# Reordered work around the half rounds of an RWKV-6 attention and expert kernel, and a fourth of the layer norm on another engine

## The reference, cut to what matters

```python
xn = layernorm(x)                            # x: 4 x 1024 x 256, float32
out = x + attention(xn) + experts(xn)

# attention, RWKV-6: 4 heads of 64
x_last = xn shifted by one token
h = tanh((xn + (x_last - xn) * miu_x) @ A)   # the codes, 5 x 32
x5 = xn + (x_last - xn) * (h @ Bp + lam)     # five mixtures: w, k, v, r, g
w = td_miu + tanh(x5[0] @ tdA) @ tdB
k = x5[1] @ Wk.T * exp(min(w, 0));  v = x5[2] @ Wv.T;  r = x5[3] @ Wr.T
g = tanh(x5[4] @ Wg1) @ Wg2
y_t[i] = sum_j r_t[j] * (S[i,j] + u[j] * k_t[j] * v_t[i])
S[i,j] = S[i,j] * exp(w_t[j]) + k_t[j] * v_t[i]
attention = (groupnorm(y) * gamma + beta) * g @ Wo.T

# experts: 8, each token goes to one
e = argmax(softmax(xn @ Wr + br))
experts = (relu(xn @ W1[e] + b1[e]) @ W2[e] + b2[e]) * max_prob
```

## Time and profile before

| | before |
|---|---|
| median of 3 runs | 611.93 us (611.58 to 612.84) |
| the profiled execution: its time, its span | 612.62 us, 611.3 us |
| PE busy | 545.2 us, 89% of the span |
| PE's weight loads busy | 483.0 us, 79% |
| DVE busy | 449.7 us, 74% |
| ACT busy | 339.4 us, 56% |
| POOL busy | 187.7 us, 31% |
| PE in the chain that ended last | 61% of the span |

### The profile page before, as it was taken

One profiled execution on the slowest core, in us unless ns is written; L12 is line 12 of the kernel. 1 busy time (PEld: TensorE's weight loads), 2 busy tenths in 40 slices (PEclk: granted clock), 3 DMA queues, 4 the chain that ended last, 5 costly groups with the idle time before them and its releaser, 6 DMA issues.

```text
span 611.3 us, 18795 instructions
## 1 busy us (share of the span) xinstructions
PE 545.2 (89%) x7278; PEld 483.0 (79%) x7278; DVE 449.7 (74%) x1124; ACT 339.4 (56%) x753; POOL 187.7 (31%) x148
## 2 busy tenths in 40 slices
PE   2779797979999999999999899999999999989974
PEld 2557686868888888889798788888897988878873
DVE  6979999978577685948576876859485767768552
ACT  4874663245655656564645456575646465554751
POOL 4401010121243252344342332523433423423233
PEclk9998898989999999999999999999999999999998
DMA  8969543895333314142342223241432433221233
GB/s 282 280 239 300 157 126 97 257 358 130 71 53 85 46 39 97 34 96 46 70 70 72 44 71 45 53 81 35 95 45 74 66 72 46 53 35 33 26 51 43
DMA packets 49802, 60.75 MB, mean 99 GB/s; under 512 B 5057, under 2 KB 44098, under 8 KB 49570
## 3 DMA queue, kind: packets, MB, share of 16 engines
q1 hardware_dynamic: 36898, 44.72, 25.6%
q0 software_dynamic: 11840, 14.42, 15.7%
q10 hardware_dynamic: 976, 0.41, 0.2%
HBM read 40.79 MB, written 23.07 MB: 104 GB/s over the span
## 4 chain that ended last, share of the span: by engine, by line
PE 61%; DVE 17%; issue 8%; ACT 7%; DMA 3%; POOL 1%; ACTq 1%; DVEq 0%; SPq 0%; POOLq 0%
PE F L656 11%; PE F L664 8%; PE G L465 7%; PE LL L524 7%; PE G L497 4%; PE G L481 4%; PE YB L589 3%; DVE mix L1016 3%; PE G L434 2%; PE YB L587 2%; ACT AT L1473 2%; DMA out<-rows,dst_row 2%; PE YB L625 1%; DVE small L815 1%; PE YB L615 1%
## 5 line engine op out<-in xcount | busy, mean ns | idle before, releaser
L1730 POOL DMA_INDIRECT out<-rows,dst_row x39 | 65.5, 1681 | 237.8 <-DVE rows L1145 226.4
L656 PEld LDWEIGHTS F<-xsT,w1s 128*128 128x128 f32 x624 | 73.8, 192 | 22.1 <-ACT xsT L1515 12.2
L656 PE MATMUL F<-xsT,w1s 128*128 128x128 f32 x624 | 78.0, 278 | 14.3 <-ACT xsT L1515 9.8
L1016 DVE SCALAR_TENSOR_TENSOR mix<-G,vec,ba 128x256 f32<-128x256 f32 x160 | 69.6, 476 | 19.1 <-PE G L434 19.1
L664 PE MATMUL F<-w,hsT 128*128 x312 | 75.1, 383 | 1.0 <-issue 0.6
L1077 DVE TENSOR_TENSOR RK<-RK,D 128x256 f32<-128x256 f32 x112 | 47.2, 421 | 35.4 <-issue 27.1
L1533 ACT ACTIVATE hsT<-F,b1c 128x128 f32<-128x128 f32 x156 | 44.5, 368 | 50.8 <-PE F L656 50.8
L664 PEld LDWEIGHTS F<-w,hsT 128*128 128x128 f32 x312 | 57.1, 190 | 9.4 <-issue 1.5
L1055 DVE COPY_PREDICATED AP_<-msk,LL 128x256 f32<-128x256 uint32 x96 | 51.1, 532 | 15.1 <-issue 11.1
L1024 DVE TENSOR_TENSOR mix<-mix,xnT 128x512 f32<-128x512 f32 x80 | 55.1, 689 | 1.5
L1716 POOL DMA_INDIRECT rows<-xn_d,src_row x39 | 40.5, 1039 | 36.5 <-PE F L645 19.6
(11 more groups left out here) (180 smaller groups left out, 1203.3 us busy)
## 6 DMA issues: line engine op xcount, KB each, us to landing
cd<-cd_d SPq DMA_DIRECT2D x30, 320.0 KB, 5.5
w<-in_W SPq DMA_DIRECT2D x16, 512.0 KB, 8.1
cd_d<-w SPq DMA_DIRECT2D x32, 160.0 KB, 2.9
b2t<-in_b SPq DMA_DIRECT2D x39, 128.0 KB
w<-in_x SPq DMA_DIRECT2D x8, 512.0 KB, 9.7
xn_d<-w SPq DMA_DIRECT2D x8, 512.0 KB
out<-in_x SPq DMA_DIRECT2D x8, 512.0 KB, 5.3
out<-res POOLq DMA_DIRECT2D x16, 256.0 KB, 4.7
```

The lines of the kernel that those rows point to most:

```text
L656: i1 = pe.matmul(FB[:, k * P:(k + 1) * P], w1s[:, cc, k, :], xsT[:, cc, :], start=(cc == 0), stop=(cc == 1))
L1016: i1 = dve.scalar_tensor_tensor(mixed_in(u, c, n, cc), bk[:, cc * UN:(cc + 1) * UN], cvec(LAM + CC * n, cc), ba[:, cc, :, :].rearrange("p ...
L1730: pool.indirect_dma_start(io["out"], bass.IndirectOffsetOnAxis(dst_row[:, f:f + 1], 0), ys[:, f % 2, :], None, compute_op=ALU.add).then_in ...
```

## The change

Six things are changed. The layer norm's fourth tile of each group is normalised on POOL and no longer on DVE, with a semaphore of its own (`xnp`) for all who read the tile. On ACT, `tokens(fa)` comes ahead of `spread`, and `bonus` behind `decay_down`; both stood at the end of the half round before. On PE, `read_out` stands ahead of `decay_down` in the halves without `fa`, and in `last_levels` the block's products come behind the two levels. On DVE, level 4 is joined by levels 2 and 3 behind `expert_out(fb)`, and `gated` comes behind `added(u, c + 1, 4)`. ACT's `saved(*v, 32)` comes ahead of `last_bias(fc)`. SP loads the bias of tile 0 ahead of W2 and waits for the experts' numbers (`ex`) first.

```diff
@@ tensor_program
                 pe.wait_ge(s["gr"], NGROW * q + 6)
+                saved_level(u, 5, LEAF)
+                saved_level(u, 6, WIDE)
                 for cc in range(CC):
...
-                            pe.matmul(pairs[0:LEAF, (h * CC + cc) * UB + b, 0:LEAF], K[rows, u, cc, b, 0:LEAF],
+                            i1 = pe.matmul(pairs[0:LEAF, (h * CC + cc) * UB + b, 0:LEAF], K[rows, u, cc, b, 0:LEAF],
                                       R[rows, u, cc, b, LEAF:P], start=True, stop=True, tile_position=(HEAD * h, 0))
-                saved_level(u, 5, LEAF)
-                saved_level(u, 6, WIDE).then_inc(s["lev"])
+                i1.then_inc(s["lev"])
...
                 if fa is not None:
                     hidden(fa)
+                else:
+                    read_out(u, c, 0)
+                    read_out(u, c, 1)
                 decay_down(u, c + 1)
                 state(u, c)
                 mixed(u, c + 1, 2)
-                read_out(u, c, 0)
-                read_out(u, c, 1)
+                if fa is not None:
+                    read_out(u, c, 0)
+                    read_out(u, c, 1)
@@ vector_program
-                for t in (2, 3):
-                    i1 = dve.tensor_scalar(xtok[:, 4 * j + t, :], xall[:, 4 * j + t, :], mv[:, t, 0:1], rs[:, t:t + 1], ALU.subtract, ALU.mult)
-                i1.then_inc(s["xnd"])
+                dve.tensor_scalar(xtok[:, 4 * j + 2, :], xall[:, 4 * j + 2, :], mv[:, 2, 0:1], rs[:, 2:3], ALU.subtract, ALU.mult).then_inc(s["xnd"])
...
                 mixed(u, c + 1, 4)
-                levels(*v, 2, 3)
                 grow(*v, 16)
                 if fb is not None:
                     expert_out(fb)
-                levels(*v, 4)
-                gated(u, c)
+                levels(*v, 2, 3, 4)
                 grow(*v, 32)
                 added(u, c + 1, 4)
+                gated(u, c)
                 grow(*v, 64)
@@ scalar_program
                 if fa is not None:
                     tokens(fa)
+                spread(u, c)
+                if fa is not None:
                     last_bias(fa)
                 key_back(u, c)
                 if fa is not None:
                     rectified(fa)
                 decay_down(u, c + 1)
-                if h == 1:
-                    bonus(0, 1)
+                bonus(*v)
...
+                saved(*v, 32)
+                if fc is not None:
                     last_bias(fc)
-                saved(*v, 32)
                 receptance(u, c + 1)
...
                 out(u, c)
-                if h < NU - 3:
-                    spread(*v)
-                    bonus(u, c + 1)
@@ gpsimd_program
+            def normalise(j):
+                st, mv, rs, nm = moments_of(j)
+                pool.wait_ge(s["rs"], j + 1)
+                pool.tensor_scalar(xtok[:, 4 * j + 3, :], xall[:, 4 * j + 3, :], mv[:, 3, 0:1], rs[:, 3:4], ALU.subtract, ALU.mult).then_inc(s["xnp"])
...
             for j in range(NJ):
                 inverse_deviation(j)
+                normalise(j)
@@ sync_program
+            sp.wait_ge(s["ex"], 1)
+            bias(0)
             sp.wait_ge(s["inv"], 1)
             for e in range(E):
                 sp.dma_start(w2[:, e * HC * C:(e + 1) * HC * C].rearrange("p (c n) -> p c n", c=HC),
                              io["W2"][e].rearrange("(c p) n -> p c n", p=P)).then_inc(s["ew2"], 16)
-            sp.wait_ge(s["ex"], 1)
-            bias(0)
```

More of the change, by code:

```diff
@@ L182, in program @@
         s = {n: ctx.enter_context(nc.semaphore("s_" + n)) for n in (
-            "cv cn c1 c2 w x0 x1 x2 x3 x4 x5 x6 x7 xk ck0 ck1 ck2 z_pool omx bn ag ve rs nm xna xnd tr tc sc lg xx hm h hi lo "
+            "cv cn c1 c2 w x0 x1 x2 x3 x4 x5 x6 x7 xk ck0 ck1 ck2 z_pool omx bn ag ve rs nm xna xnd xnp tr tc sc lg xx hm h hi lo "
             "four hg hf hc cx ls lgc lgt bst cst wvc ew1 ew2 "
@@ L338, in ln_transpose @@
                 pe.wait_ge(s["xnd"], j + 1)
+                pe.wait_ge(s["xnp"], j + 1)
                 if j == 0:
@@ L819, in moments @@
                     dve.wait_ge(s["xna"], j - 1)
+                    dve.wait_ge(s["xnp"], j - 1)
                 for t in range(4):
@@ L1345, in scaled @@
                     act.wait_ge(s["xnd"], NJ)
+                    act.wait_ge(s["xnp"], NJ)
                 for cc in range(CC):
@@ L1352, in scaled_half @@
                 act.wait_ge(s["xnd"], NJ - 1)
+                act.wait_ge(s["xnp"], NJ - 1)
                 for cc in range(CC):
@@ L1657, in scalar_program @@
             block(1, 0)
-            spread(1, 0)
             for h in range(1, NU - 2):
@@ L1852, in sync_program @@
                 sp.wait_ge(s["xnd"], j + 1)
+                sp.wait_ge(s["xnp"], j + 1)
                 sp.dma_start(xkr[j, :, :, :], xtok[:, 4 * j:4 * j + 4, :]).then_inc(s["xk"], 16)
```

## The result

The changed kernel takes 593.64 us (median of 4 runs, 591.82 to 594.24), the kernel before, run beside it, 612.38 (4 runs, 611.58 to 614.2): a ratio of 0.9685, 95% interval 0.9653 to 0.9717. The forecast was 599.5 with a range from 595.0 to 605.0. The profiled execution took 594.24 us with a span of 592.9, so the span lost 18.4 us where I had summed 12.4.

What follows compares the result with a forecast made beforehand. PE was taken to bound the half rounds and DVE the front. The terms 9.7 + 2.3 + 2.0 - 1.6 give 12.4 us, which off the median of 611.93 is 599.5 us, range 595 to 605.

Steps and rivals of the forecast that it cites:

- ACT's order: Halves with `fa`: copying the tokens first removes PE's 0.97 us wait ahead of `hidden(fa)` ten times, 9.7 us gained.
- Rival A: `fa` halves: the wait moves on to late `bonus` or power; 3.4 us gained, 608.5; chance 0.15 shared with another rival.
- DVE's order: Half rounds: earlier `expert_out(fb)` removes PE's 0.23 us wait ahead of `hidden(fc)` ten times, 2.3 us gained.
- rival B: `last_levels`: PE's `issue` waits at the small products vanish, up to 5.1 us less, 594.4 to 597; chance 0.12.
- `gated`: DVE in the half rounds: moved back some 1.3 us, but PE asks for it two microseconds later, so nothing.
- The block: `last_levels`: the same 80 products behind the two levels, 0; bounds 5.1 us gained or 5.1 lost.
- The read-out: PE in halves 1, 7 and 13: earlier read-out lengthens a half by 0.3 us, half 1 by about 1.0; 1.6 lost.
- The front: Layer norm: one tile less on DVE saves 0.33 us for each of six groups, 2.0 us, from 1 to 3.
- rival C: Layer norm: if POOL's tile takes over 1.1 us, POOL sets the pace; slower, 620 at 4 us; chance 0.04.
- W2: Loads moved some 4 us later still have 14 us to land, so 0; at most 4 us if slack is gone.

Runs made afterwards that it cites:

- e1: Changed kernel with ACT's `spread` and `bonus` back at the end of the half round before, ahead of the tokens' copy: 606.2 us, 0.9873 of the kernel before.
- e7: Kernel before with DVE's new order in the half rounds alone: 606.12 us, 0.986 of the kernel before.
- e2: Changed kernel with DVE's order of before (levels 2 and 3 ahead of `expert_out(fb)`, `gated` ahead of `added`): 605.97 us, 0.9869 of the kernel before.
- e17: Changed kernel with POOL's subtraction for the unit after next waiting for `grow(64)`: 588.2 us, 0.9755 of the kernel before.
- e13: Changed kernel with levels 2 and 3 ahead of `grow(16)` and `expert_out(fb)` again, `gated` left late: 594.96 us, 0.9872 of the kernel before.
- e10: Kernel before with the block's products behind the two levels and nothing else changed: 605.3 us, 1.0024 of the kernel before.
- e14: Changed kernel with `gated` between level 4 and `grow(32)`, and POOL's subtraction waiting for `grow(64)`: 596.11 us, 0.9869 of the kernel before.
- e9: Changed kernel with `gated` back between level 4 and `grow(32)`: 616.44 us, 1.0204 of the kernel before.
- e3: Changed kernel with the block's products ahead of the two levels again: 592.69 us, 0.9645 of the kernel before.
- e12: Changed kernel with the block's products first, the read-out late in all halves and W2 ahead of tile 0's bias: 583.83 us, 0.9657 of the kernel before.
- e4: Changed kernel with the read-out behind mixture 2 again in halves 1, 7 and 13: 593.52 us, 0.9645 of the kernel before.
- e8: Changed kernel with the block's products ahead of the levels and the read-out late in halves 1, 7 and 13: 588.23 us, 0.9594 of the kernel before.
- e16: e12's kernel again, W2 ahead of tile 0's bias, run beside e15: 584.4 us, 0.9664 of the kernel before.
- e15: e8's kernel again, W2 behind tile 0's bias, run beside e16: 586.6 us, 0.9707 of the kernel before.
- e5: Changed kernel with two tiles of each layer-norm group normalised on DVE again and none on POOL: 599.98 us, 0.9777 of the kernel before.
- e6: Changed kernel with W2 loaded ahead of tile 0's bias again: 593.99 us, 0.9683 of the kernel before.
- e18: e12's kernel with POOL's subtraction waiting for `grow(64)`: 583.84 us, 0.9684 of the kernel before.

## Why the prediction was off

- **ACT's order, 9.7 us forecast.** The mechanism was right (e1). The size was not: 1.17 us a half and not 0.97. The step that failed was the sizing by the idle time printed ahead of the product: that was 2.0 us of the miss. From start to start had 1.57 us, and four transposes without a wait behind them take 0.43. Rival A, a wait that moves on, did not come: no wait on `Ru`, `yn` or the power stands in PE's list of after.
- **DVE's order, 2.3 us forecast.** This is the term most off, and the main reason why the time fell below the range: 0.91 a half (e7), some 9 to 10 us over the halves. Two steps failed. I sized the wait by the printed 0.23 where the distance gives 0.39. And I took the `issue` waits at the small products for a thing by itself, to be had by the block's order if at all (rival B). They went with DVE's order, 0.43 to 0.48 us a half in those groups (e2, e7). So B's gain came in part, by another edit; what these short waits are is not known (e17). e13 and e10 leave open how much of it depends on what differs between the groups of runs.
- **`gated`, at nothing.** I named the cover, that PE asks for it two microseconds later, but looked only at who wants `gated`, not at what stands behind it. In the changed kernel `grow(32)` ends at 224.81 and PE begins at 224.96: 0.15 us of slack. Without the move 0.60 us a half would have been given back (e14), and 2.2 with the clash (e9: 4.07 us from `hidden(fc)` to `last_levels` against 1.88).
- **The block, at 0.** Right on the kernel before (e10), but the changed one loses 0.20 us a half by it (e3), some 2 us. I saw no reason for it, and the runs show none.
- **The read-out, -1.6.** Half 7: forecast 0.3, measured 0.14 to 0.16 (e12, e4), with a wait of 1.06 us ahead of `decay_up`, which I had put at 0.9. Half 1: forecast 1.0, but the pairs e4 to the result and e8 to e3 give 1.6 and 4.0 us, and the clock is mixed into both. By its low time (3.5 us less, 10.3 more), at the 0.25 us for each that e4 and e8 suggest (36.45 - 34.52 less the block's 0.2, over 6.9 us), the read-out itself costs 1.4 to 2.5. That is a weak estimate: one and the same kernel has a half 1 of 31.94 us in e12 and 33.07 in e16, neither with a stretch at the lower clock, and another 34.52 in e8 with 6.8 us of it and 36.02 in e15 with 3.4. When the clock falls there, and for how long, I can't forecast.
- **The front, 2.0.** Measured 2.6 and 2.7 at the shifted tokens (against the kernel before and against e5) and 2.8 at the mark of half 1, where runs with the same front lie as far apart as 130.67 (e8) and 132.52 (e4). The tile on POOL took 1.23 us, past the 1.1 of rival C's threshold, so that POOL sets the pace, as the rival said; at 2.35 us a group it is still 0.29 us faster than before. Of the 2.6 us the groups gave 1.6 (the last tile starts at 24.63, its two at 26.26 before); the rest comes from that tile, which takes 0.41 us where the two took 1.97. The bound was right and its comparison wrong: I measured POOL against DVE's new pace, and not against the old one, which is what decides on slower.
- **W2, at 0.** Right for this kernel (e6), with the loads where I had put them (the last starts at 136.5). The slack is gone in a faster one: 1.8 of the 2.5 us that PE stands there (e15), within the bound of 4.

Summed by what was measured: 11.7 + 9.1 for ten halves, less 2.0 for the block, plus 2.8 for the front, less 3.6 for half 1, plus 0.5 for half 7 and 0.8 at the end is 19.3, 0.9 above the 18.4 by which the span fell; a tenth of a microsecond in each half is shared by the parts or not accounted for.

## What to carry to other kernels

Size a stall by the distance between the starts of two instructions, and compare it with the same pair where nothing waits; the printed idle time gave 0.97 for 1.14 and 0.23 for 0.39. For an operation that is moved, ask what stands behind it at its old and at its new place, and what runs on POOL at that time: the same `gated` cost nothing, 0.6 or 2.2 us a half. Such a place can also be lost by an edit elsewhere: e5 and e7 met the clash in half 7 without touching it. A kernel with all edits but the block's and the read-out's is faster than the changed one: e8, at 0.9594 in its group, and e12 with W2 first besides, which had the lowest time of its group.

## What the runs showed of the hardware that was not expected

- POOL's tensor_scalar of 128 x 256 takes 1.23 us, more than its subtraction of 128 x 512 from two inputs, 1.05 (the changed kernel).
- A DVE multiplication of 128 x 256 with both inputs in SBUF is held from 0.42 to 2.00 us by a POOL subtraction of 1.05 us that starts 0.66 us behind it (e9); with the subtraction moved it takes 0.41 (e14). A much smaller one, 128 x 8, is held from 0.16 to 1.75 us (half 7 of e5 and e7).
- PE's 80 small products of `last_levels` take from 1.52 us (e12) to 2.73 (e2, half 1) at the full clock. They differ by the order of the lists, by the group of runs and by the half: 2.07 in half 10 of the kernel before and 2.32 in its half 11, with POOL's subtraction 1.2 us behind the start in both. The cause is not known; POOL's subtraction is not it alone (e17).
- The time at the lower clock in half 1 went from none (e12, e16, e18) to 17.1 us (e3) in kernels that differ in a few edits, and PE was at it also while busy for 2.00 of 2.00 us.
- The kernel before took 614.0 us in one group of runs and 604.3 in the next, on a chip of the same number, while e8's kernel went from 588.2 to 586.6 between groups. Why stays open.
